# A graph attention layer on one core: the last pair of steps in pieces of 13, 9 and 4, the 99th count from the neighbour, four small gathers in the pause

## The chip, the cores and the metric

One core of a Trainium2 chip. The metric is the device time of one execution in microseconds, as the median of several runs. In the traces POOL is GpSimd, DVE is VectorE, ACT is ScalarE, PE is TensorE and SP the sync engine, which here only issues DMAs.

## What is computed

One pre-norm graph attention layer, 12,500 nodes of 128 features, 412,500 edges sorted by destination, 4 heads of 32. Cut to what matters:

```python
h = relu(layernorm(x)) @ W_node.T                       # 12500 x 4 x 32
e = edge_attr @ W_edge.T                                # 412500 x 4 x 32
att = leaky_relu(sum(concat(h[src], h[tgt], e) * a))    # 412500 x 4
m = maximum(segment_max(att, tgt), 0)
ex = exp(att - m[tgt])
denom = segment_sum(ex, tgt) + (num_edges - deg) * exp(-m)
out = x + segment_sum(ex / denom[tgt] * h[src], tgt)
```

## The kernel before

The edges are dealt to 128 partitions in order, T = 3224 each, so that a partition goes through its edges as through a sequence, one "step" per edge. A segment (all edges of one destination) is a run of steps; the running maximum and the decayed running sums are scans along the steps, and the state after a segment's last edge is the segment's result. At a partition's first and last segment the neighbours must be joined.

**Head.** For each of 98 columns of nodes (node p·98+w stands in partition p, column w) the kernel needs `cnt`, the number of edges whose destination lies below that node. ACT counts over 512 chunk ends (`count_chunks`), POOL gathers the chunk concerned (98 columns and a 99th, whose count is only needed as the upper end of the last column), DVE counts within it (`count_within`). `positions` makes from the counts the degrees, `put_i` (where a node's target term is scattered to, POOL's 98 scatters) and `get_i` (where a node's result is read). It is called for columns 0 to 90 and then for the last 7. Between them `project_copy` takes the projections of 7 columns of nodes at a time from PE's banks; SP stores these rows (`rows_scratch`), 136 numbers per node: for each head 32 values and a one, then 4 source terms. A store's buffer is one of two, so group g+2 waits for store g.

**Loop.** 13 steps are a block (KB), two blocks a pair (PB = 26), 124 pairs. For each pair POOL issues 26 indirect gathers of 128 rows into `slots`; each gather is one instruction. DVE waits for all 26 (`gather_dma`), does `logits` (source term + target term + edge term, leaky relu, running maximum M by a scan, the exponents D and D2), then for each block `sums`: multiply the gathered rows by the weights into V, and scan V with the decays A. ACT gives the weights and the decays by exponentials and copies V and M into R; SP stores R as the states of the pair (`state_scratch`). The last pair (`at_end`) goes in two pieces of 13 steps with semaphores of their own (`gather_end`), so that its first half is worked on while the second is still gathered.

**Tail.** When all states are stored, POOL gathers each partition's first state (`s_first`) and for the 98 columns the state at each node's last edge (`get_i`), 7 to a group; DVE divides, adds x, SP stores. Beside it DVE and PE join the segments that cross partitions (`tail_views`, from the last column of V and M). The queues are written out by hand per engine; every wait is on a semaphore. What POOL waits for between the last gather of the loop and the first of the tail stands in these lines:

```python
pool.wait_ge(flags_done, 1)
pool.wait_ge(zero_stored, 16)
for k in range(2):
    pool.wait_ge(store_dma[k], STORES[k])
pool.wait_ge(val_done, BLOCKS)
gather(s_first[:, :], state_d[:, :], fe_i[:, 0:1], fix_gather)
```

## Time and profile before

| | |
|---|---|
| median of 3 runs | 4960.86 us (4958.59 to 4969.13) |
| the profiled execution, its own time | 4962.95 us |
| its span in the trace | 4955.9 us |
| POOL busy | 3712.2 us, 75% |
| DVE busy | 2412.0 us, 49% |
| ACT busy | 1368.3 us, 28% |
| PE busy | 777.3 us, 16% |
| DMA | 627.97 MB, 127 GB/s in the mean |

Busy time is that of the instructions on an engine; the span runs from the first to the last instruction of the program. The 7 us between the span and the execution's own time lie before and behind it. An engine's instruction and the DMA that it issues are two things: a gather on POOL is busy while its descriptors are made, and lands later.

### The profile page before, as it was taken

What the parts mean: (1) busy time and instruction counts of PE and PEld (TensorE: products, weight loads), DVE (VectorE), ACT (ScalarE), POOL (GpSimd) and SP (SyncE); (2) the same over time, 40 slices, a digit from 0 to 9 for tenths busy, and PEclk for the clock granted to TensorE, in tenths of its full rate; (3) what the DMA queues carried; (4) which work ended last, traced back from release to release, by engine and by line L of the source; (5) the groups of instructions that cost most, each with busy time, mean ns of one, the idle gap of its engine ahead of it and who ended that gap; (6) DMA issues with size and microseconds to landing.
All of it is one profiled execution on the core that took longest, in us unless ns stands there. A gap on an engine that the chain in (4) does not pass through costs nothing.

```text
span 4955.9 us, 14358 instructions
## 1 busy us (share of the span) xinstructions
PE 777.3 (16%) x1453; PEld 390.6 (8%) x1453; DVE 2412.0 (49%) x2384; ACT 1368.3 (28%) x1021; POOL 3712.2 (75%) x3530
## 2 busy tenths in 40 slices
PE   5321111111111111111111111111111111111100
PEld 3310000000000000000000000000000000000000
DVE  7337454545445454454544545445454454544543
ACT  7013232222322222222222322223222232222320
POOL 6667777777777777777777777777777777777766
PEclk9555555555555555555555555555555555555555
DMA  7234444343443434434344343433434434343353
GB/s 250 90 132 119 140 123 128 114 137 114 126 125 114 137 114 128 123 115 137 114 127 123 114 136 114 129 121 115 137 114 128 122 115 136 114 131 120 116 170 104
DMA packets 171831, 627.97 MB, mean 127 GB/s; under 512 B 72897, under 2 KB 73666, under 8 KB 155426
## 3 DMA queue, kind: packets, MB, share of 16 engines
q0 software_dynamic: 115936, 252.37, 21.0%
q1 hardware_dynamic: 55874, 375.39, 20.1%
q14 instruction: 17, 0.14, 0.0%
q8 instruction: 4, 0.07, 0.0%
HBM read 382.66 MB, written 244.86 MB: 127 GB/s over the span
## 4 chain that ended last, share of the span: by engine, by line
POOL 70%; issue 24%; another core or an unknown queue 2%; ACT 2%; DVE 1%; PE 0%; DMA 0%; POOLq 0%; ACTq 0%; DVEq 0%; SPq 0%
POOL slots L308 69%; ACT pen L375 1%; DVE pen L482 0%; PE ae L792 0%; DVE slots L496 0%; ACT big L392 0%; ACT slots L391 0%; POOL tdst_scratch L311 0%; ACT R L421 0%; PE wexp L785 0%; DMA state_scratch<-R 0%; DVE V L636 0%; DVE slots L501 0%; DMA cols<-in_cols_dram 0%
## 5 line engine op out<-in xcount | busy, mean ns | idle before, releaser
L308 POOL DMA_INDIRECT slots<-rows_scratch,idx x3224 | 3421.5, 1061 | 1066.5 <-issue 1066.5
L803 PE MATMUL ae<-eab,w_att 128*128 128x416 f32 x992 | 650.6, 829 | 3796.2 <-DMA eab<-in_ea_dram 2539.1
L603 DVE TENSOR_TENSOR z<-slots,big 128x104 f32<-128x104 f32 (+1 forms) x125 | 43.1, 345 | 2116.3 <-DMA slots<-rows_scratch,idx 1887.3
L636 DVE TENSOR_TENSOR_SCAN V<-A,V 128x1848 f32<-128x1848 f32 x248 | 993.7, 4007 | 35.4 <-issue 4.8
L421 ACT COPY R<-V 128x1716 f32<-128x1716 f32 x248 | 777.8, 3136 | 339.1 <-DVE V L636 196.7
L417 ACT ACTIVATE A<-D 128x1848 f32<-128x1848 f32 x246 | 419.7, 1706 | 744.7 <-DVE V L636 410.3
L803 PEld LDWEIGHTS ae<-eab,w_att 128*128 128x128 f32 x992 | 296.0, 313 | 4150.4 <-issue 3384.4
L626 DVE TENSOR_TENSOR V<-slots,wexp 128x1716 f32<-128x1716 f32 x125 | 404.8, 3239 | 22.4 <-issue 21.0
L626 DVE TENSOR_TENSOR V<-slots,extra 128x1716 f32<-128x1716 f32 x123 | 398.2, 3237 | 22.0 <-issue 16.3
L438 ACT ACTIVATE wexp<-D 128x104 f32<-128x104 f32 x62 | 16.2, 261 | 1092.5 <-DVEq L621 628.8
L438 ACT ACTIVATE extra<-D 128x104 f32<-128x104 f32 x61 | 15.9, 261 | 1063.2 <-DVEq L621 631.2
L308 POOL DMA_INDIRECT V<-in_dst_dram,chunk_i x99 | 97.0, 979 | 56.6 <-issue 28.1
L311 POOL DMA_INDIRECT tdst_scratch<-tnode,put_i x98 | 95.2, 972 | 50.5 <-issue 30.0
L482 DVE TENSOR_SCALAR_CACHE_REDUCE pen<-V,cols 128x806 bf16<-128x806 int16 x99 | 100.8, 1050 | 34.7 <-DMA V<-in_dst_dram,chunk_i 24.1
L308 POOL DMA_INDIRECT slots<-state_scratch,get_i x98 | 92.8, 947 | 29.9 <-issue 29.9
L633 DVE COPY V<-V 128x132 f32<-128x132 f32 x247 | 79.4, 322 | 11.3
L646 DVE STREAM_TRANSPOSE ae_t<-ae 128x416 f32<-128x416 f32 x124 | 73.4, 592 | 0.9 <-issue 0.6
L375 ACT ACTIVATE pen<-last_b,half_n 128x512 bf16<-128x512 f32 x99 | 70.0, 713 | 9.3 <-issue 9.3
L496 DVE TENSOR_TENSOR slots<-ae,rstd 128x384 f32<-128x384 f32 x28 | 15.5, 552 | 104.3 <-remote 89.9
L612 DVE TENSOR_TENSOR_SCAN M<-pen,att 128x108 f32<-128x108 f32 (+1 forms) x123 | 47.4, 385 | 19.6 <-issue 19.1
L792 PE MATMUL ae<-w_ext,big 128*128 128x136 f32 x168 | 39.3, 416 | 86.5 <-DVE tnode L502 53.9
L608 DVE TENSOR_TENSOR z<-z,ae_t 128x104 f32<-128x104 f32 (+1 forms) x125 | 42.3, 339 | 9.3
(168 smaller groups left out, 602.3 us busy)
## 6 DMA issues: line engine op xcount, KB each, us to landing
state_scratch<-R SPq DMA_DIRECT2D x123, 1768.0 KB
eab<-in_ea_dram SPq DMA_DIRECT2D x126, 832.0 KB
slots<-rows_scratch,idx POOLq DMA_INDIRECT x3224
rows_scratch<-slots SPq DMA_DIRECT2D x14, 476.0 KB
tdst_scratch<-eab SPq DMA_DIRECT2D x4, 1612.0 KB
big<-tdst_scratch SPq DMA_DIRECT2D x8, 806.0 KB
big<-in_x_t_dram SPq DMA_DIRECT2D x14, 448.0 KB, 4.3
big<-in_x_dram SPq DMA_DIRECT2D x7, 896.0 KB
```

The lines of the kernel that those rows point to most:

```text
L308: pool.indirect_dma_start(buf, None, table, bass.IndirectOffsetOnAxis(ap=index, axis=0)).then_inc(done, 16)
L311: pool.indirect_dma_start(table, bass.IndirectOffsetOnAxis(ap=index, axis=0), buf, None).then_inc(done, 16)
L375: nc.scalar.activation(junk_a[k % 9], last_b[:, :], ACT.Sign, bias=half_n[:, k:k + 1], scale=-1.0, accum_out=sgn[:, k:k + 1])
L417: nc.scalar.activation(a_all.rearrange("p (h v t) -> p h v t", h=H, v=HB), d2.rearrange("p h (a t) -> p h a t", a=1).broadcast_to([P, H, H ...
L421: return nc.scalar.copy(R[:, k, v * KB:(v + 1) * KB, 0:VAL], vcols(v)[:, :, 1:COL].rearrange("p c t -> p t c"))
L482: nc.vector.tensor_scalar(junk_v[k % RING], ring[:, k % RING, :], cols[:, k:k + 1], None, ALU.is_lt, ALU.add, accum_out=within[:, k:k + 1] ...
L612: nc.vector.tensor_tensor_scan(M[:, u, 0:H * (n + 1)], pen_u.rearrange("p a h t -> p (a h t)"), a[:, 0:H * (n + 1)], 0.0, ALU.min, ALU.max)
L626: nc.vector.tensor_tensor(v4[:, :, :, 1:COL], slots[:, a:a + KB, 0:VAL].rearrange("p t (h v) -> p h v t", h=H), w4.rearrange("p h (a t) -> ...
L633: nc.vector.tensor_copy(vcols(v)[:, :, 0:1], vcols(1 - v)[:, :, KB:COL])
L636: nc.vector.tensor_tensor_scan(V[:, v, :], a_all, V[:, v, :], 0.0, ALU.mult, ALU.add).then_inc(scanned, 1)
L646: nc.vector.transpose(ae_t[:, :], ps_ae[k][:, 0:KB * Q]).then_inc(ae_taken, 1)
L803: last = mm(ps_ae[k][:, 0:KB * Q], w_att[:, a * P:(a + 1) * P], eab[:, k, a * KB * Q:(a + 1) * KB * Q], start=a == 0, stop=a == 3)
```

## The change

Three parts. (1) The last pair goes in three pieces, 13, 9 and 4 steps (`LAST`); `logits`, `sums`, `decay` and `copy_sums` take a piece's offset and length, the buffers for the ends get a third part, a third store is issued, and the tail reads the last piece's end. (2) The loop over counts runs over 98 columns; the 99th entry of `cnt` is copied from the first entry of the next partition by a DMA from SBUF to SBUF (for the last partition it is the constant E), and DVE waits for it in the second `positions`. (3) Behind the loop's gathers POOL issues four more gathers, of 124, 120, 112 and 64 rows, into a new tile `t_again`, and waits for them; nothing reads that tile.

```diff
+LAST = ((0, KB), (KB, 9), (KB + 9, KB - 9))
-COUNTS = (0, 2, 4, 7, 12, 20, 29, 38, 47, 56, 65, 74, 83, 92, 99)
+COUNTS = (0, 2, 4, 7, 12, 20, 29, 38, 47, 56, 65, 74, 83, 92, 98)
+PARTIAL = (124, 120, 112, 64)
...
+            sp.wait_ge(put_ready, 1)
+            sp.dma_start(cnt[0:P - 1, W:W + 1], cnt[1:P, 0:1]).then_inc(next_count, 16)
             for g in range(STEPS):
...
-                    for v in range(2):
-                        sp.wait_ge(copied, p + 1 + v)
-                        a, b = (p * 2 + v) * (KB * ROW), (p * 2 + v + 1) * (KB * ROW)
-                        sp.dma_start(state_rows[:, a:b], R[:, 1, v * KB:(v + 1) * KB, :].rearrange("p t r -> p (t r)")).then_inc(store_dma[1], 16)
+                    for e, (o, n) in enumerate(LAST):
+                        sp.wait_ge(copied, p + 1 + e)
+                        a = (p * PB + o) * ROW
+                        sp.dma_start(state_rows[:, a:a + n * ROW], R[:, 1, o:o + n, :].rearrange("p t r -> p (t r)")).then_inc(store_dma[1], 16)
...
-            for k in range(W + 1):
+            for k in range(W):
                 if k in COUNTS:
...
+            for k, n in enumerate(PARTIAL):
+                gather(t_again[0:n, k, :], tnode_d[:, :], first_i[0:n, 0:1], again_dma)
+            pool.wait_ge(again_dma, 16 * len(PARTIAL))
             pool.wait_ge(flags_done, 1)
...
             for h in range(H):
-                nc.scalar.activation(pen_end[:, :, h, 1:COL], pen_a[:, T - PB:T].rearrange("p (b t) -> p b t", t=KB), ACT.Relu)
+                for e, (o, n) in enumerate(LAST):
+                    a = T - PB + o
+                    nc.scalar.activation(pen_end[:, e, h * (n + 1) + 1:(h + 1) * (n + 1)], pen_a[:, a:a + n], ACT.Relu)
...
+                    for e, (o, n) in enumerate(LAST):
+                        act.wait_ge(d_ready, p + 1 + e)
+                        u = (p + e) % 2
+                        nc.scalar.activation(w_exp[u][:, 0:H * n], D1[:, u, 0:H * n], ACT.Exp).then_inc(w_ready, 1)
+                        decay(hk(D2_end[:, e, 0:H * (n + 1)]), n + 1)
...
+                        act.wait_ge(scanned, 2 * p + 1 + e)
+                        copy_sums(1, o, e % 2, n).then_inc(copied, 1)
...
             def positions(a, b, c):
...
+                if b == W:
+                    dve.wait_ge(next_count, 16)
                 nc.vector.tensor_tensor(deg[:, a:b], cnt[:, a + 1:b + 1], cnt[:, a:b], ALU.subtract)
```

The order of the instructions changes at three places. On SP's queue, where the head ends, before:

```order
L251 DMA idx<-in_src_dram 128x52
L255 DMA tdst_scratch<-eab 128x3224 [waits centre_done,filled]
L255 DMA tdst_scratch<-eab 128x3224 [waits centre_done] x3
L258 DMA rows_scratch<-slots 128x952 [waits rows_ready] x7
L262 DMA eab<-in_ea_dram 128x1664 [waits tdst_filled]
```

and in the changed kernel:

```order
L257 DMA idx<-in_src_dram 128x52
L261 DMA tdst_scratch<-eab 128x3224 [waits centre_done,filled]
L261 DMA tdst_scratch<-eab 128x3224 [waits centre_done] x3
L263 DMA cnt<-cnt 127x1 [waits put_ready]
L266 DMA rows_scratch<-slots 128x952 [waits rows_ready] x7
```

The copy of the counts stands ahead of all stores of the projected rows (`rows_scratch`), and waits for DVE's first `positions`.

On POOL between the loop and the tail, before (`x_first`, `rest_first` and `s_first` are one gather each, for the joins):

```order
L308 DMA slots<-rows_scratch,idx 128x136 x25
L308 DMA x_first<-in_x_dram,first_i 128x128 [waits rest_stored]
L308 DMA rest_first<-rest_scratch,first_i 128x1
L308 DMA s_first<-state_scratch,fe_i 128x136 [waits store_dma1,store_dma0,val_done,zero_stored,flags_done]
L308 DMA slots<-state_scratch,get_i 128x136 x49
```

and in the changed kernel:

```order
L316 DMA slots<-rows_scratch,idx 128x136 x25
L316 DMA x_first<-in_x_dram,first_i 128x128 [waits rest_stored]
L316 DMA rest_first<-rest_scratch,first_i 128x1
L316 DMA t_again<-tnode_scratch,first_i 124x4
L316 DMA t_again<-tnode_scratch,first_i 120x4
L316 DMA t_again<-tnode_scratch,first_i 112x4
L316 DMA t_again<-tnode_scratch,first_i 64x4
L316 DMA s_first<-state_scratch,fe_i 128x136 [waits store_dma0,store_dma1,zero_stored,val_done,flags_done,again_dma]
L316 DMA slots<-state_scratch,get_i 128x136 x49
```

The four gathers stand ahead of the waits for the stores, and the first gather of the tail waits for them too.

On DVE the end of the last pair, before (from the second piece's logits):

```order
L603 TENSOR_TENSOR z<-slots,big 128x52 [waits gather_end1]
L608 TENSOR_TENSOR z<-z,ae_t 128x52
L610 SCALAR_TENSOR_TENSOR att_end<-z 128x4x13
...
L626 TENSOR_TENSOR V<-slots,wexp 128x132x13 [waits w_ready]
L633 COPY V<-V 128x132
L636 SCALAR_TENSOR_TENSOR V<-A,V 128x1848 [waits a_ready]
L676 COPY V<-V 128x128 [waits copied]
```

and in the changed kernel, the second and the third piece:

```order
L623 TENSOR_TENSOR z<-slots,big 128x36 [waits gather_end1]
...
L647 TENSOR_TENSOR V<-slots,wexp 128x132x9 [waits w_ready]
L655 COPY V<-V 128x132
L658 SCALAR_TENSOR_TENSOR V<-A,V 128x1320 [waits a_ready]
L623 TENSOR_TENSOR z<-slots,big 128x16 [waits gather_end2]
...
L647 TENSOR_TENSOR V<-slots,extra 128x132x4 [waits copied,w_ready]
L655 COPY V<-V 128x132
L658 SCALAR_TENSOR_TENSOR V<-A,V 128x660 [waits a_ready]
L705 COPY V<-V 128x128 [waits copied]
```

What came in one piece of 13 comes in two, of 9 and 4, each with its logits, multiply and scan, and each waits for its own gathers.

## Rows read from the trace of the kernel before

**Rows 1.** The page: chain that ended last by engine, and costliest group.

```profile
POOL 70%; issue 24%; another core or an unknown queue 2%; ACT 2%; DVE 1%; PE 0%; DMA 0%; POOLq 0%; ACTq 0%; DVEq 0%; SPq 0%
...
L308 POOL DMA_INDIRECT slots<-rows_scratch,idx x3224 | 3421.5, 1061 | 1066.5 <-issue 1066.5
```

**Rows 2.** Windows: stretch, length, busy PE, PEld, DVE, ACT, POOL, PEclk, DMA share, GB/s.

```profile
3228.03:3519.23 291.20, 43.34 (x65) 19.88 (x66) 141.20 (x120) 80.62 (x48) 221.52 (x209) 0.55 0.40 123
3519.23:3810.58 291.35, 39.70 (x64) 18.37 (x64) 140.76 (x120) 80.59 (x48) 219.03 (x209) 0.56 0.40 123
3300.61:3337.71 37.10, 8.22 (x14) 3.96 (x13) 17.52 (x15) 10.07 (x6) 28.62 (x27) 0.55 0.39 121
3591.81:3628.76 36.95, 7.35 (x15) 3.46 (x13) 17.84 (x15) 10.08 (x6) 27.57 (x26) 0.61 0.40 121
305.75:4793.76 4488.01, 642.30 (x976) 291.99 (x976) 2210.17 (x1890) 1250.24 (x746) 3421.53 (x3224) 0.55 0.41 125
```

**Rows 3.** Windows: the tail's gathers on POOL, first to last.

```profile
4814.15:4937.75 123.60, 0.78 (x3) 0.47 (x3) 41.68 (x86) 3.96 (x18) 93.72 (x99) 0.50 0.49 155
```

**Rows 4.** Timeline of the last pair: start, duration, instruction, idle before and its releaser.

```profile
4781.16 1.81 POOL L308 DMA_INDIRECT slots<-rows_scratch,idx  x1 [0.30 <-issue]
...
4787.32 0.95 POOL L308 DMA_INDIRECT slots<-rows_scratch,idx  x1 [0.30 <-issue]
4787.39 3.12 ACT L421 COPY R<-V 128x1716 f32<-128x1716 f32 x1 [5.75 <-issue]
...
4792.36 1.10 POOL L308 DMA_INDIRECT slots<-rows_scratch,idx  x1 [0.30 <-issue]
...
4795.16 0.95 POOL L308 DMA_INDIRECT rest_first<-rest_scratch,first_i  x1 [0.30 <-issue]
4795.57 0.25 DVE L603 TENSOR_TENSOR z<-slots,big 128x52 f32<-128x52 f32 x1 [8.21 <-DMA slots<-rows_scratch,idx]
...
4797.61 0.22 ACT L429 ACTIVATE wexp<-D 128x52 f32<-128x52 f32 x1 [7.10 <-issue]
...
4797.86 3.24 DVE L626 TENSOR_TENSOR V<-slots,wexp 128x1716 f32<-128x1716 f32 x1 [0.31 <-ACT wexp L429]
...
4801.55 4.01 DVE L636 TENSOR_TENSOR_SCAN V<-A,V 128x1848 f32<-128x1848 f32 x1
4805.60 3.14 ACT L421 COPY R<-V 128x1716 f32<-128x1716 f32 x1 [5.93 <-DVE V L636]
...
4814.15 0.94 POOL L308 DMA_INDIRECT s_first<-state_scratch,fe_i  x1 [18.03 <-DMA state_scratch<-R]
```

**Rows 5.** Chain that ended last, its step behind the last copy.

```profile
4808.76 4.49 DMA state_scratch<-R
```

**Rows 6.** DMA issues: count, KB each, median us to landing.

```profile
state_scratch<-R SPq DMA_DIRECT2D x2, 884.0 KB
...
a_sb<-in_a_blk_dram SPq DMA_DIRECT2D x1, 6.0 KB, 2.3
```

**Rows 7.** Timeline of the head, at the end of the counting.

```profile
155.07 11.02 SPq L258 DMA_DIRECT2D rows_scratch<-slots  x2
...
157.53 0.95 POOL L308 DMA_INDIRECT V<-in_dst_dram,chunk_i  x1 [0.31 <-issue]
...
160.02 0.25 DVE L517 TENSOR_TENSOR put_i<-pick,cnt 128x91 int32<-128x91 f32 x1
...
161.06 1.00 POOL L311 DMA_INDIRECT tdst_scratch<-tnode,put_i  x1 [2.59 <-issue]
...
166.83 1.05 DVE L482 TENSOR_SCALAR_CACHE_REDUCE pen<-V,cols 128x806 bf16<-128x806 int16 x1
...
167.80 1.05 DVE L482 TENSOR_SCALAR_CACHE_REDUCE pen<-V,cols 128x806 bf16<-128x806 int16 x1
...
170.52 0.55 DVE L496 TENSOR_TENSOR slots<-ae,rstd 128x384 f32<-128x384 f32 x1
```

**Rows 8.** Waits of DVE, 150 to 300 us: total us, times, longest.

```profile
DVE slots L496 <- remote: 89.9, 7, 22.2
```

More of the change, by code:

```diff
@@ L343, in body @@
                     k = q % 2 * PB + j
-                    gather(slots[:, k, :], rows[:, :], idx[:, q // 2, k:k + 1], gather_end[j // KB] if at_end(it, q) else gather_dma[q % 2])
+                    done = gather_end[sum(j >= o for o, n in LAST) - 1] if at_end(it, q) else gather_dma[q % 2]
+                    gather(slots[:, k, :], rows[:, :], idx[:, q // 2, k:k + 1], done)
             loop(pool, body)
@@ L426, in body @@
                 if at_end(it, q):
-                    for v in range(2):
-                        act.wait_ge(d_ready, p + 1 + v)
-                        nc.scalar.activation(w_exp[1 - v][:, 0:H * KB], D1[:, 1 - v, 0:H * KB], ACT.Exp).then_inc(w_ready, 1)
-                        decay(hk(D2_end[:, v, :]))
-                        if v == 0:
+                    for e, (o, n) in enumerate(LAST):
[3 more added lines that the diff above has]
+                        decay(hk(D2_end[:, e, 0:H * (n + 1)]), n + 1)
+                        if e == 0:
                             act.wait_ge(store_dma[1], 16 * (p // 2))
-                        nc.scalar.copy(R[:, 1, v * KB:(v + 1) * KB, VAL:ROW], hk(M[:, 1 - v, 0:H * COL])[:, :, 1:COL].rearrange("p h t -> p t h"))
-                        act.wait_ge(scanned, 2 * p + 1 + v)
-                        copy_sums(1, v).then_inc(copied, 1)
+                        nc.scalar.copy(R[:, 1, o:o + n, VAL:ROW], hk(M[:, M_END[e], 0:H * (n + 1)])[:, :, 1:n + 1].rearrange("p h t -> p t h"))
+                        act.wait_ge(scanned, 2 * p + 1 + e)
+                        copy_sums(1, o, e % 2, n).then_inc(copied, 1)
                     return
@@ L478, in _ @@
             dve.sem_inc(consts, 1)
+            nc.vector.memset(cnt[:, W:W + 1], float(E))
             def count_within(k):
@@ L533, in _ @@
             dve.wait_ge(loaded_lasts, 32)
-            for k in range(W + 1):
+            for k in range(W):
                 if k % RING == 0:
@@ L630, in sums @@
                 else:
-                    if v:
+                    if o:
                         dve.drain()
-                    nc.vector.tensor_copy(vcols(v)[:, :, 0:1], vcols(1 - v)[:, :, KB:COL])
+                    nc.vector.tensor_copy(vc[:, :, 0:1], before)
                 dve.drain()
                 dve.wait_ge(a_ready, ready)
-                nc.vector.tensor_tensor_scan(V[:, v, :], a_all, V[:, v, :], 0.0, ALU.mult, ALU.add).then_inc(scanned, 1)
+                nc.vector.tensor_tensor_scan(V[:, v, 0:VAL * (n + 1)], A[:, 0:VAL * (n + 1)], V[:, v, 0:VAL * (n + 1)], 0.0, ALU.mult, ALU.add).then_inc(scanned, 1)
@@ L647, in body @@
                 if at_end(it, q):
-                    for v in range(2):
-                        dve.wait_ge(gather_end[v], 16 * KB)
-                        logits(p, k, 1 - v, v, KB, att_end, att_end, pen_end[:, v:v + 1, :, :], D2_end[:, v, :])
-                        dve.wait_ge(w_ready, p + 1 + v)
-                        if v == 0:
-                            dve.wait_ge(copied, p)
-                        sums(k, v, hk(w_exp[1 - v][:, 0:H * KB]), 2 * p + 1 + v, False)
+                    for e, (o, n) in enumerate(LAST):
+                        u = (p + e) % 2
+                        c = LAST[e + 1][1] + 1 if e + 1 < len(LAST) else COL
+                        dve.wait_ge(gather_end[e], 16 * n)
+                        logits(p, k, u, M_END[e], o, n, att_end[:, e, :], hk(att_end[:, e + 1, 0:H * c]), pen_end[:, e, 0:H * (n + 1)], D2_end[:, e, 0:H * (n + 1)])
+                        dve.wait_ge(w_ready, p + 1 + e)
+                        if e != 1:
+                            dve.wait_ge(copied, p + e // 2)
+                        m = LAST[e - 1][1] if e else KB
+                        sums(k, o, n, e % 2, hk(w_exp[u][:, 0:H * n]), 2 * p + 1 + e, vcols(1 - e % 2, m + 1)[:, :, m:m + 1])
                     return
                 dve.wait_ge(gather_dma[k], it * (16 * PB * UP // 2) + 16 * PB * (q // 2 + 1))
-                logits(p, k, k, 0, PB, att, att_end if isinstance(it, int) and it == ITERS - 1 and q == UP - 2 else att, pen[:, ds(p, 1), :, :], D2[:, k, :])
+                one_before = isinstance(it, int) and it == ITERS - 1 and q == UP - 2
+                logits(p, k, k, k, 0, PB, att, hk(att_end[:, 0, :]) if one_before else hk(att[:, :]),
+                       pen[:, ds(p, 1), :, :].rearrange("p a h t -> p (a h t)"), D2[:, k, :])
                 dve.wait_ge(w_ready, p + 1)
@@ L660, in body @@
                 for v in range(2):
-                    sums(k, v, hk(w_exp[k])[:, :, v * KB:(v + 1) * KB], it * (2 * UP) + 2 * q + 1 + v, isinstance(p, int) and p == 0 and v == 0)
+                    sums(k, v * KB, KB, v, hk(w_exp[k])[:, :, v * KB:(v + 1) * KB], it * (2 * UP) + 2 * q + 1 + v,
+                         None if isinstance(p, int) and p == 0 and v == 0 else vcols(1 - v)[:, :, KB:COL])
                 if isinstance(p, int) and p < UP:
```

96 lines of the change are left out of this document (52 added, 44 removed).

## The prediction

> **What bounds the kernel now.** I read the page first. Its chain of work that ended last is POOL for 70% and "issue" for 24%, and the costliest group by far is one line, L308: 3224 indirect gathers that POOL issues back to back, 1061 ns busy and 330 ns between two [rows 1]. The window over the main loop says the same from outside: 4488.0 us with 3224 of them, 1.392 us each, while DVE is busy for 2210 us of it and ACT for 1250 [rows 2]. POOL is also what the tail waits for: 99 gathers in 123.6 us, 1.25 us each [rows 3]. So the run is a head of 305.75 us, a loop and a tail that both go at POOL's pace, and between loop and tail a pause of 18.03 us in which POOL has nothing it may issue [rows 4]. The change can move the time only in the head, in the pause, or by making POOL's own gathers cheaper or dearer.
>
> The timeline of the last pair shows what fills the pause. POOL issues the last step's gather at 4792.36; DVE starts the second half at 4795.57, ACT gives the weights at 4797.61, DVE multiplies from 4797.86 (3.24 us) and scans from 4801.55 (4.01 us), ACT copies from 4805.60 (3.14 us) [rows 4]. Then the chain has the store: issued at 4808.76, 4.49 us [rows 5], and POOL's first gather of the tail is at 4814.15 [rows 4]. From the last gather to that one all is serial, and all but the first 5.5 us scales with the number of steps in the last piece.
>
> **Part 1: pieces of 13, 9, 4.** The first piece is as before; ACT begins to copy it at 4787.39, so DVE is free then [rows 4]. Durations go by elements. Fixed in a piece: 2.29 us from the start of the logits to the multiply, and 4801.55 − 4797.86 − 3.24 = 0.45 us between multiply and scan. I take these as unchanged for smaller pieces, though their small instructions shrink a little.
> - Piece of 9: its last step (the 22nd) is gathered at 4787.32, four gathers before the last. With the 3.21 us from issue to DVE that the last one took it starts at 4790.5. It takes 2.29 + 3.24·9/13 + 0.45 + 4.01·9/13 (1320 elements of 1848 is 10/14, 2.86) = 7.8 us, and ends at 4798.4.
> - Piece of 4: its gathers landed at 4795.57, so it waits for DVE and starts at 4798.4. DVE would be ready to multiply at 4800.7. ACT stands first in line with the copy of the piece of 9 (3.14·9/13 = 2.2 us, to 4800.6), then gives the weights; the multiply starts about 4800.85. 3.24·4/13 = 1.0, 0.45, 4.01·5/14 = 1.4: scanned at 4803.7. ACT's copy is 3.14·4/13 = 1.0: 4804.7.
> - Its store is 272 KB where 884 KB took 4.49 us [rows 5, 6]. The bounds: the gather of 128 rows of 544 bytes took 3.21 − 0.95 = 2.3 us from its end to DVE [rows 4], and 4.49. The size is nearer to the gather's 68 KB, so I take 2.8 us, by a straight line between them. The store of the piece of 9 is issued at 4800.6 and is over by 4805.1 even at 4.49. Landed: 4807.5. POOL resumed 0.9 us behind the landing before (4814.15 − 4808.76 − 4.49), so now at 4808.4.
> - The term: 4808.4 − 4814.15 = **−5.7 us**, from −4.1 (store of 4.49) to −7 (store of 2.3, and the small instructions shorter by 0.6). What follows (x loaded again, the DVE chain of the joins) hangs on the same two events and moves with them.
>
> The cost is a third set of eight small DVE instructions, a copy, a weight activation and a third store issue. All lie inside the 7.8 + 5.3 us just counted. ACT's eight more activations for the penalties (128x4 to 128x13) stand in front of the loop, where DVE's first logits wait for POOL's 26th gather; at 1.39 us each that is some 35 us of cover.
>
> **Part 2: four gathers in the pause.** POOL is free at 4795.16 + 1.25 = 4796.4. Four at 1.25 end at 4801.1 and land 2.3 later, 4803.4. The store lands at 4807.5, so 4.1 us of cover: each of the four may be 1 us dearer before POOL's wait on them is the last. Cost **0**. Nothing reads what they fetch. Their rows are not multiples of 128, which no row shows; at the price of a gather they cost 0, and at that of the dear one at 4781.16 (1.81 us and 0.3 [rows 4]) the four land at 4807.1, again 0; only beyond that do they show.
>
> **Part 3: the 99th column.** It takes away one gather of POOL in the head (157.53 was the last; POOL then waits until 161.06 for the positions anyway [rows 7], so 0), one Sign activation, and one count of DVE, which takes 0.97 us from start to next start and stands directly ahead of the positions of the last 7 columns and of the projection copies that feed POOL's scatters [rows 7]. It adds a copy of 127 elements from SBUF to SBUF on SP's queue, issued when the first positions are ready (160.3), and DVE waits for it from about 168.4 (its last count started at 167.80, now 0.97 earlier, and two small instructions follow). Before, the nearest transfers from their issue to their landing are 2.3 us (6 KB) and 4.49 (the store) [rows 5, 6]: landed by 162.6 to 164.8, hidden with 3.6 us to spare. Queued behind it on SP is the store of the first 7 columns of rows, which was issued at 155.07 [rows 7] and now goes out at about 160.8. DVE needs that buffer for the third group, at 170.52 less the 0.97 [rows 7], 169.5; 8.7 us against 4.49 for a larger store: hidden. So **−1.0 us**, between −1.4 and +6: the head has seven waits of DVE on something the trace doesn't name, 89.9 us in all [rows 8], and a reordering there can make one longer.
>
> A rule of the Trainium skill speaks against this copy ("DMA: Bandwidth & Descriptors", section on why a DMA increments its semaphore by 16): the engines used are the largest number up to 16 that divides the outer size, so 127 partitions all go on one engine. The trace has no DMA of 127 partitions. At 10.5 ns a packet, from the same page's section on bandwidth and so an estimate, 127 make 1.3 us, less than the cover, so the sum would stay.
>
> **The sum.** −5.7 − 1.0 = −6.7 us on the profiled execution's 4962.95 gives 4956.2. The median of the runs is 2.1 us lower, so 4954.2. That is 0.135%; a measurement of this kernel tells about 0.2%, 9.9 us, from no change.
>
> **What could decide instead: the loop.** The change takes one of the gathers ahead of the loop away, so each of the 3224 is one place earlier in POOL's own count. That this place matters is visible. Eight pairs (208 gathers) take 291.20 and 291.35 us in two stretches one behind the other, and within each of them one pair takes 37.10 and 36.95 [rows 2], where the other seven of 291.20 average 36.30. The pairs start at even places only (26 is even, 198 gathers stand before them); with 197 they all start at odd ones, which this trace never shows. On average over places I expect nothing, 0. One slow pair more or less in eight is 0.8 · 123/8 = 12.3 us.
>
> **The rivals.**
> - *The odd places are kinder*: no slow pair, −12.3 − 6.7, 4942. For it: the slow pair is a coincidence of one start place with the stretch where DVE begins the next pair; against it: I see only even places. From −3.2 us in the loop on (a quarter of a slow pair) the result is beyond 0.2%. Chance 0.28.
> - *They are unkinder*: one slow pair more in eight gives +12.3 − 6.7, 4966.5, no measurable change; 0.08. Three slow in eight, +24.6 − 6.7, give 4978.8, **slower**; it decides from +16.6 us in the loop, 1.1 us per eight pairs. Nothing in the rows speaks for that much. Chance 0.05.
> - *The tail pays for the four gathers*: if the odd row counts leave POOL's gathers of the tail as dear as the loop's, 1.392 instead of 1.248 [rows 2, 3], 99 of them cost +14.3, and the sum is 4968.5. Against it: the loop's surcharge goes with other engines' work there and the tail is flat now. Chance 0.04.
> - *The pause doesn't shrink*: the piece of 4 is bound by something else (the store of the piece of 9 still under way, the four gathers slow), only −1.0 remains, 4960. Chance 0.05.
> - The forecast: 0.50.
>
> **Numbers.** Range 4942 to 4966: from the kinder loop to one slow pair more; below lie perhaps 0.08, above 0.1. Faster by over 0.2%: 0.30 (the first rival, and the low end of my terms). Within: 0.64. Slower: 0.06.
>
> **What would show it.** POOL's idle before the tail's first gather, 18.0 before, is 12.3 less the four gathers' 5.0 us; DVE's scan of the last piece at 1.4 us; a store of the last 4 steps landing under 3 us; the cnt copy landed before DVE asks. The loop's window, first to last gather of 3224, tells the rest: 4488 within 3 us if I am right. Wrong would be a loop off by over 5 us, a gather in the tail above 1.3 us, or a first loop gather later than 305.

## The result and the profile after

The changed kernel is slower, by a hair: the ratio of its time to the kernel before is 1.0017, 95% interval 1.0009 to 1.0025, so 4.5 to 12.4 us; medians 4978.66 against 4967.99 us, 13 runs each. I had forecast 4954 and a range to 4966. Seven of those 24.5 us are not the change's: the forecast started from the median of 3 runs of the kernel before (4960.86), and 13 runs put it at 4967.99. The profiled execution took 4971.35 us against 4962.95, 8.4 us more; its span is 4969.5 us against 4955.9, 13.6 more. The other 5.2 us come back outside the span: the time of an execution less its span was 7.1 us before (6.6 to 7.6 in the runs of the kernel before, on the chips where it takes 4967 us or more) and is 1.8 now. No instruction is recorded there, so what shrinks is not shown, but a tail that ends 13 us later makes the kernel only some 8 us slower.

The 13.6 us between the spans split at landmarks of PoolE (POOL in the rows: GpSimd). "The loop's last gather" is the end of the last of the 3224 gathers, 4793.46 before and 4793.11 after (4791.87 + 1.24); all times with a plus below are counted from it, in every kernel.

| us | before | after |
|---|---|---|
| first loop gather | 305.75 | 304.04 |
| loop, to the end of its last gather | 4487.71 | 4489.06 |
| s_first gathered | +20.69 | +18.37 |
| TensorE's first transpose of the ends | +13.52 | +25.96 |
| last operation of the first rows' correction (x_first) starts | +49.05 | +63.75 |
| first to last of the tail's 98 gathers | 121.41 | 125.74 |
| last scatter | +152.79 | +166.14 |

The "correction" is VectorE's work on x_first, the rows of the segments that cross partitions; the "last scatter" writes these rows and is PoolE's last instruction with data. The head gave 1.7 us here, the loop took 1.35 and the end 13.35.

The windows of the changed kernel, columns as in [rows 2, 3]: the loop, and the tail's 99 gathers.

```profile
304.04:4793.41 4489.37, 637.97 (x976) 290.98 (x976) 2222.01 (x1900) 1252.78 (x751) 3418.33 (x3224) 0.55 0.41 125
4811.47:4939.97 128.50, 2.32 (x9) 1.42 (x9) 38.76 (x87) 3.87 (x18) 95.52 (x99) 0.50 0.46 143
```

The loop is the same within 1.4 us of 4488.01. The timeline of the changed kernel's third piece and pause (start, duration, instruction, idle before):

```profile
4797.75 0.17 DVE L637 COPY att_end<-M 128x4 f32<-128x4 f32 x1
4797.96 0.99 POOL L316 DMA_INDIRECT t_again<-tnode_scratch,first_i  x1 [0.30 <-issue]
...
4800.53 0.92 POOL L316 DMA_INDIRECT t_again<-tnode_scratch,first_i  x1 [0.30 <-issue]
4801.56 0.17 DVE L639 SCALAR_TENSOR_TENSOR D_end<-pen_end,dm 128x16 f32<-128x16 bf16 x1 [3.64 <-issue]
4802.94 0.19 ACT L444 ACTIVATE extra<-D 128x16 f32<-128x16 f32 x1 [3.99 <-DVEq L642]
...
4805.75 1.53 DVE L658 TENSOR_TENSOR_SCAN V<-A,V 128x660 f32<-128x660 f32 x1 [1.11 <-issue]
4807.32 1.15 ACT L435 COPY R<-V 128x528 f32<-128x528 f32 x1 [3.41 <-DVE V L658]
...
4808.54 0.17 DVE L714 MEMSET R<- 4x129 f32 x1
...
4811.47 0.95 POOL L316 DMA_INDIRECT s_first<-state_scratch,fe_i  x1 [10.02 <-DMA state_scratch<-R]
```

Three times between 4797.9 and 4805.7 VectorE stands idle at a drain for no reason that the profile names ("issue"): 3.6, 1.2 and 1.1 us. (A drain is an instruction that waits until the engine's earlier ones are through.) In the last piece of the kernel before none of them did. The pause shrinks by 2.3 us instead of 5.7. The next drain is far worse. TensorE waits for it:

```profile
4819.07 0.47 PE L840 MATMUL ae<-ident,V 128*128 128x128 f32 x1 [98.75 <-issue]
```

The memset at 4808.54 ended at 4808.71; TensorE starts 10.4 us later. Before, the same drain let TensorE begin at 4806.97, 0.1 us behind the last memset. From there VectorE stays late. Its last part, one group of seven columns, looks like this:

```profile
4856.86 0.29 DVE L768 TENSOR_TENSOR x_first<-x_first,R 128x128 f32<-128x128 f32 x1 [1.11 <-issue]
...
4871.86 0.18 DVE L776 TENSOR_TENSOR R<-R,rest 128x28 f32<-128x28 f32 x1
4874.36 0.21 DVE L778 TENSOR_TENSOR R<-R,slots 128x28 f32<-128x28 f32 x1 [2.31 <-issue]
4875.76 0.34 DVE L780 RECIPROCAL wexp<-R 128x28 f32<-128x28 f32 x1 [1.19 <-issue]
4876.47 1.09 DVE L783 TENSOR_TENSOR A<-slots,wexp 128x896 f32<-128x896 f32 x1 [0.38 <-issue]
4877.86 1.09 DVE L789 TENSOR_TENSOR big<-big,A 128x896 f32<-128x896 f32 x1 [0.30 <-issue]
4878.87 0.18 DVE L776 TENSOR_TENSOR R<-R,rest 128x28 f32<-128x28 f32 x1
```

A group takes 7.00 us, of which 2.9 are work, and 14 groups behind a correction at 4857 make 4955. PoolE's last gather is long over by then:

```profile
4954.86 1.09 DVE L789 TENSOR_TENSOR big<-big,A 128x896 f32<-128x896 f32 x1 [0.30 <-issue]
...
4959.25 1.01 POOL L319 DMA_INDIRECT out_dram<-x_first,fix_i  x1 [19.27 <-DMA out_dram<-big]
```

The kernel before has groups of 7.00 us too, but its correction was over 14 us sooner, so it caught up with the gathers: its last three groups, from 4922 on, each start within 0.1 us of the end of ACT's exponentials, and these wait for the gathers. These rows of before show its end:

```profile
4842.51 0.29 DVE L739 TENSOR_TENSOR x_first<-x_first,R 128x128 f32<-128x128 f32 x1 [1.11 <-issue]
...
4946.25 1.00 POOL L311 DMA_INDIRECT out_dram<-x_first,fix_i  x1 [8.50 <-DMA out_dram<-big]
```

So the tail has changed hands: PoolE sets its end before, VectorE after.

### The profile page after: what moved, and what is told of

Read it like the earlier page. It is cut to its first block, busy times and chain, and to the rows that moved or that the text cites. A ratio compares the mean times of both kernels' runs of the same rounds, so it can differ in the third digit from the quotient of the medians.

```text
span 4969.5 us, 14393 instructions
## 1 busy us (share of the span) xinstructions
PE 769.4 (15%) x1453; PEld 388.4 (8%) x1453; DVE 2420.8 (49%) x2394; ACT 1369.3 (28%) x1031; POOL 3714.2 (75%) x3533
## 4 chain that ended last, share of the span: by engine, by line
POOL 70%; issue 24%; ACT 2%; another core or an unknown queue 2%; DVE 1%; PE 1%; DMA 0%; POOLq 0%; DVEq 0%; ACTq 0%; SPq 0%
POOL slots L316 70%; ACT pen L387 1%; DVE pen L499 0%; PE ae L821 0%; PE wexp L814 0%; DVE slots L513 0%; PE A L804 0%; ACT big L404 0%; ACT slots L403 0%; POOL tdst_scratch L319 0%; DVE V L658 0%; DVE slots L518 0%; ACTq L388 0%; PE wexp L821 0%
## 5 line engine op out<-in xcount | busy, mean ns | idle before, releaser
L658 DVE TENSOR_TENSOR_SCAN V<-A,V 128x1848 f32<-128x1848 f32 (+1 forms) x249 | 994.1, 3992 | 36.4 <-issue 5.9
L435 ACT COPY R<-V 128x1716 f32<-128x1716 f32 (+1 forms) x249 | 778.0, 3125 | 345.7 <-issue 191.9
L647 DVE TENSOR_TENSOR V<-slots,wexp 128x1716 f32<-128x1716 f32 (+1 forms) x125 | 403.9, 3232 | 22.4 <-issue 21.4
```

The lines of the kernel that those rows point to most:

```text
L435: return nc.scalar.copy(R[:, k, o:o + n, 0:VAL], vcols(v, n + 1)[:, :, 1:n + 1].rearrange("p c t -> p t c"))
L647: nc.vector.tensor_tensor(vc.rearrange("p (h v) t -> p h v t", h=H)[:, :, :, 1:n + 1], slots[:, a:a + n, 0:VAL].rearrange("p t (h v) -> p ...
L658: nc.vector.tensor_tensor_scan(V[:, v, 0:VAL * (n + 1)], A[:, 0:VAL * (n + 1)], V[:, v, 0:VAL * (n + 1)], 0.0, ALU.mult, ALU.add).then_inc ...
```

## The experiments

Heads differ from run to run by more than the effects (the kernel before's first loop gather and that of kernels with its head lay between 299 and 324 us), so I read the distances from the loop's last gather beside each ratio. Where the change's end is unchanged (after, early_exit, after_again) they repeat to 0.15 us. Where the end is that of the kernel before they repeat less well: s_first lies between +19.43 and +20.69 in before, tail20, drains20 and head_loop, the last scatter of before, drains20 and head_loop between +152.20 and +152.79. A ratio moves less than the last scatter where VectorE ends late, for the 5 us outside the span.

**First four: which part, and per what.** two_pieces and no_partials are the changed kernel less one part (in two_pieces the tail also reads the ends from where two pieces leave them); tail20 and early20 the kernel before plus 20 tiny memsets of VectorE.

```diff
 two_pieces:  LAST = ((0, KB), (KB, KB))
 no_partials:
-            for k, n in enumerate(PARTIAL):
-                gather(t_again[0:n, k, :], tnode_d[:, :], first_i[0:n, 0:1], again_dma)
-            pool.wait_ge(again_dma, 16 * len(PARTIAL))
 tail20, on before:
             dve.drain().then_inc(end_packed, 1)
+            for k in range(20):
+                nc.vector.memset(spare[:, k:k + 1], 0.0)
 early20, on before, at the end of VectorE's body():
+                if isinstance(it, int) and it == ITERS - 1 and q == UP - 3:
+                    for m in range(20):
+                        nc.vector.memset(spare[:, m:m + 1], 0.0)
```

> The changed kernel with the last pair again in two pieces of 13 steps; the four gathers and the new source of the 99th count stay. It takes 19 instructions of VectorE's own (the third piece) out of the end. Theory A (pace): after the loop VectorE's drains end on a grid of 0.70 us and one group of nine instructions takes 7.00 us, whatever PoolE does, so VectorE gets through the code behind the loop at about one instruction in 0.70 us or a little more; the third piece costs 19 x 0.70 = 13.3 us of it. Then the correction of the first rows ends near 4843 to 4845 instead of 4857.1, PoolE's idle time before the last scatter is 8 to 10 us instead of 19.3, and the time is that of the kernel before within 4 us (ratio 0.999 to 1.001). Theory B (the four gathers held VectorE up and it never caught up): the correction still ends 10 us or more late and the ratio stays near 1.0017.

> The changed kernel without the four gathers of 124, 120, 112 and 64 rows and the wait for them. Theory A (pace of VectorE behind the loop): no instruction of VectorE goes away, so its drains in the third piece still take about 5.8 us more than they need, s_first is gathered near 4811, the last scatter starts near 4959 after 18 to 20 us of idle, and the ratio stays 1.001 to 1.0025. Theory B (the four gathers hold VectorE's drains up): the third piece runs through without those 5.8 us, s_first is gathered at 4805.5 to 4808, the last scatter starts 10 us or more earlier and the ratio is 0.998 to 1.000.

> The kernel before with 20 memsets of 128x1 on VectorE, with no drain between them, behind the drain that tells TensorE that the ends are packed. By their length they cost 20 x 0.13 = 2.6 us, of which 1.7 us lie in a wait for TensorE. Theory A (pace per instruction): the correction of the first rows ends 20 x 0.70 = 14 us later (4856 to 4858 instead of 4842.8), VectorE does not catch up with the gathers any more, and the last scatter starts 10 to 13 us later: ratio 1.002 to 1.003. Theory C (only drains are slow, whatever stands between them): correction 0 to 3 us later, same time within 2 us.

> The kernel before with the same 20 memsets of 128x1 on VectorE, at the end of the last pair but two, where VectorE waits some 10 us for the next gathers. Theory A with a store of instructions that refills while VectorE waits: nothing changes, the first slow drain stands at the same line as before (two drains behind the masks' scans) and the ratio is 0.999 to 1.001. Theory D (what matters is where a block of 128 instructions ends, so anything that shifts the code makes the end slower): the first slow drain moves 20 instructions up, into the last piece, and the time grows by 5 to 13 us, as if a third piece stood there.

| | s_first | x_first | 98 gathers | last scatter | ratio (95%) |
|---|---|---|---|---|---|
| before | +20.69 | +49.05 | 121.41 | +152.79 | |
| after | +18.37 | +63.75 | 125.74 | +166.14 | 1.0017 (1.0009 to 1.0025) |
| two_pieces | +20.62 | +49.05 | 124.04 | +155.76 | 1.0009 (1.0000 to 1.0018) |
| no_partials | +18.36 | +63.75 | 121.35 | +166.63 | 1.0018 (1.0009 to 1.0027) |
| tail20 | +19.60 | +77.05 | 124.49 | +176.08 | 1.0039 (1.0025 to 1.0052) |
| early20 | +22.00 | +60.15 | 121.24 | +162.59 | 1.0008 (0.9997 to 1.0019) |

two_pieces puts the correction back to +49.05 exactly: the third piece costs 14.7 us there. What is left of its last scatter, 3.0 us, goes with its 98 gathers, 2.6 us longer than before. no_partials changes neither s_first nor the correction. Its third piece shows the same idle time while PoolE does nothing, so the four gathers don't cause it:

```profile
4810.90 0.17 DVE L636 SCALAR_TENSOR_TENSOR D_end<-pen_end,dm 128x16 f32<-128x16 bf16 x1 [3.58 <-issue]
...
4820.79 0.95 POOL L316 DMA_INDIRECT s_first<-state_scratch,fe_i  x1 [15.56 <-issue]
...
4828.40 0.48 PE L837 MATMUL ae<-ident,V 128*128 128x128 f32 x1 [97.60 <-issue]
```

tail20 shows the thing itself. VectorE's timeline of its memsets:

```profile
4815.14 0.15 DVE L689 MEMSET spare<- 128x1 f32 x4
4815.62 0.20 DVE L689 MEMSET spare<- 128x1 f32 x6 [0.33 <-issue]
4817.84 0.06 DVE L689 MEMSET spare<- 128x1 f32 x1 [2.02 <-issue]
4819.94 0.06 DVE L689 MEMSET spare<- 128x1 f32 x1 [2.04 <-issue]
4820.64 0.06 DVE L689 MEMSET spare<- 128x1 f32 x1 [0.65 <-issue]
4822.04 0.06 DVE L689 MEMSET spare<- 128x1 f32 x1 [1.34 <-issue]
...
4829.05 0.06 DVE L689 MEMSET spare<- 128x1 f32 x1 [1.34 <-issue]
4830.45 0.06 DVE L689 MEMSET spare<- 128x1 f32 x1 [1.34 <-issue]
```

Ten come in a burst, the others at distances of 0.70, 1.40 and 2.10 us. They do nothing and cost the correction 28.0 us, 1.40 each, twice what I expected. early20 falls between my two theories: where they ran they came in a burst, and still the correction came 11.1 us later, and the first slow drains stand in the two pairs that followed. I read this as a lead that the memsets used up and that was not won back in two pairs; no row shows such a lead itself.

**Second four: fewer instructions, another exit, drains, other places.**

```diff
 wide, on after: VectorE's last part, ACT's exponentials and the stores
+WIDE = ((0, 2), (2, 2), (4, 2), (6, 1), (7, 2), (9, 2), (11, 2), (13, 1))
-            for g in range(STEPS):
+            for c, (g, m) in enumerate(WIDE):
 early_exit, on after:
-            with eng.Fori(1, ITERS - 1) as it:
+            with eng.Fori(1, ITERS - 2) as it:
 drains20, on before: dve.drain() in place of tail20's memsets
 head_loop, on before: the 20 memsets before targets(0), and in the loop after each second pair
```

> The changed kernel with VectorE's last part in 8 groups of 14 columns (two of 7, because the slots wrap at 49) instead of 14 groups of 7: the same elements, 54 instructions fewer on VectorE. In the changed kernel this part is nine instructions and 7.00 us a group, 98 us for 14 groups behind a correction that ends at 4857.1, and that makes the end (4955). Theory A (VectorE is late because each of its instructions behind the loop takes a step of 0.70 us or more): 72 instructions take 8 x 7.0 = 56 us, VectorE catches up with the gathers near 4915, and the last scatter comes 9.5 us behind the last gather as in the kernel before: 150 to 153 us after the loop's last gather instead of 166.1; ratio to the kernel before 0.998 to 1.000. Theory E (VectorE is slow by elements): groups take twice as long and nothing is gained, ratio 1.0017.

> The changed kernel with the loop left one iteration sooner: the last 8 pairs of steps stand written out instead of the last 4, nothing else differs. Theory A1 (from the exit on, instructions come at some 1.1 us each without a limit ahead, and VectorE's 134th or so is the first that is not there in time): four pairs of 36 us use 25 instructions each, that is 100 x 1.1 = 110 of 145 us, so the end starts some 35 us further ahead, the slow drains of the last piece and of the first 30 instructions behind it go, and the last scatter comes 12 us or more sooner: ratio 0.997 to 0.999. Theory A2 (VectorE works off a store of a fixed size that refills at this pace while it waits): the slow drains stand where they stood, ratio 1.001 to 1.0025.

> The kernel before with 20 drains where the 20 memsets stood (behind the drain that tells TensorE that the ends are packed). There is nothing to drain after the first, so each takes some 0.03 us by itself. Theory A (pace per instruction, whatever it does): as the memsets, the correction ends 14 to 28 us later than the 49.05 us after the loop's last gather of the kernel before, ratio 1.002 to 1.004. Theory F (memsets are a case of their own, 1.4 us each): 0 to 3 us later, ratio 1.000.

> The kernel before with 20 memsets of 128x1 on VectorE at two other places: before the first pair of steps (written out, before the loop) and after the second pair of each turn of the loop. Read is only the distance from one to the next. Theory A in its narrow form (only code written out behind the loop comes slowly): 0.01 to 0.05 us at both places. In its wide form (all code that is not in a loop comes at 0.70 us or more once the store is used up): near 0.01 in the loop, and 0.7 to 1.4 us for the last ones of the 20 before it.

| | x_first | 98 gathers | last scatter | ratio (95%) |
|---|---|---|---|---|
| wide | +63.84 | 125.65 | +155.22 | 1.0012 (1.0003 to 1.0021) |
| early_exit | +63.75 | 125.74 | +166.15 | 1.0021 (1.0012 to 1.0031) |
| drains20 | +49.05 | 121.16 | +152.20 | 1.0000 (0.9990 to 1.0009) |
| head_loop | +49.11 | 121.48 | +152.48 | one run |

With wide groups (8.4 us for twice the elements) VectorE catches up and 10.9 of the 13.4 us come back: VectorE's last part decides what the lateness costs, and that part goes by instructions more than by elements. Where the loop is left changes nothing. drains20 refutes my pace "per instruction, whatever it does", as far as the correction goes: it comes at +49.05 as before. But the drains did not pass at once. In drains20, and the last line in before:

```profile
4828.02 0.17 DVE L685 MEMSET R<- 4x129 f32 x1
4838.24 0.29 DVE L692 TENSOR_SCALAR V<-ae 128x128 f32<-128x128 f32 x1 [10.05 <-issue]
...
4864.16 0.29 DVE L741 TENSOR_TENSOR x_first<-x_first,R 128x128 f32<-128x128 f32 x1 [1.10 <-issue]
```

```profile
4808.55 0.29 DVE L690 TENSOR_SCALAR V<-ae 128x128 f32<-128x128 f32 x1 [1.66 <-PE ae L815]
```

Thirteen of the drains pass within 1.5 us, the others stand 0.70 to 2.8 us apart, and the first instruction behind them starts at +23.13 instead of +15.09. By +40 the 8 us are made up, where the 20 memsets' 28.0 us stay. So for what is lost in the end instructions with data count: a group's five at 7.00 us are 1.40 each, like the memsets; the third piece's eleven at 1.40 would be 15.4, measured 14.7. That is a count that fits, not a cause. head_loop: in the loop the 20 stand in one burst; before it the first 12 do, and the last come 0.7 us apart, half the price of those behind the loop, as here:

```profile
307.13 0.33 DVE L640 MEMSET spare<- 128x1 f32 x12
308.29 0.07 DVE L640 MEMSET spare<- 128x1 f32 x2 [0.83 <-issue]
309.73 0.06 DVE L640 MEMSET spare<- 128x1 f32 x1 [1.37 <-issue]
310.44 0.06 DVE L640 MEMSET spare<- 128x1 f32 x1 [0.65 <-issue]
```

**Third four: is it code that comes for the first time? And what do the four gathers cost?** looped writes VectorE's last part as two loops of seven turns (its waits for x stand ahead of the loops, and its products have one buffer instead of two); full4 has PARTIAL = (P, P, P, P); two kernels leave the four gathers out.

```diff
 looped, on after:
-            for g in range(STEPS):
+            for half in range(2):
+                with dve.Fori(0, 7) as g:
+                    group(half, g)
```

> The changed kernel with VectorE's last part (14 groups of 7 columns, the same instructions and sizes) written as two loops of seven turns instead of 14 times over. Theory A (code that VectorE meets for the first time comes at about 1.4 us for each instruction with data once the store is used up, code of a loop's later turns does not: in the main loop 20 memsets stood 0.01 us apart): the correction still ends 63.8 us after the loop's last gather, the first turn of each loop takes some 7 us, later ones 3.5 to 5 us, VectorE catches up with the gathers before 4900 and the last scatter comes at 151 to 155 instead of 166.1; ratio 0.999 to 1.001. Theory G (VectorE is held up by PoolE's gathers and the transfers, whatever code it runs): 7.0 us a group as before, last scatter at 166, ratio 1.0017.

> The changed kernel with four gathers of 128 rows in place of those of 124, 120, 112 and 64. In the changed kernel the 98 gathers of the end take 125.7 us, without the four gathers 121.35. Theory R (the row counts leave the rings of descriptors uneven): here 121.4, as without them. Theory O (it is the place of the 98 gathers in the row of all gathers, or their start against VectorE's, which four more of any size shift as well): 124 to 126. The time is VectorE's either way (last scatter at 166), ratio 1.0017.

> The changed kernel with the 8 wide groups on VectorE and without the four gathers: pieces of 13, 9 and 4 and the new count stay. If the last part is PoolE's again, s_first comes 18.4 us after the loop's last gather (before: 20.7), the 98 gathers take 121.4 (wide with the four gathers: 125.7), and the last scatter stands 9.4 us behind the last gather: 18.4 + 1.2 + 121.4 + 9.4 = 150.4 against 152.8 before, ratio 0.9990 to 1.0003. Had the four gathers nothing to do with the 4.3 us, it stays at 154 to 155, ratio 1.0005.

> The changed kernel with VectorE's last part as two loops and without the four gathers. As for the wide groups: 150 to 151 us from the loop's last gather to the last scatter if code of a loop comes without delay and the four gathers cost the 4.3 us, ratio 0.9990 to 1.0003; 166 if VectorE stays at 7.0 us a group.

| | x_first | 98 gathers | last scatter | ratio (95%) |
|---|---|---|---|---|
| looped | +63.75 | 141.67 | +196.82 | 1.0079 (1.0066 to 1.0092) |
| full4 | +63.75 | 126.29 | +166.15 | 1.0024 (1.0015 to 1.0034) |
| wide_no_partials | +63.75 | 121.18 | +151.91 | 0.9997 (0.9988 to 1.0006) |
| looped_no_partials | +63.75 | 141.95 | +192.16 | 1.0070 (1.0057 to 1.0083) |

looped went the wrong way by 31 us. A turn of its first loop (the first three take 7.4, 10.8 and 14.8 us) and one of its second, on VectorE:

```profile
4911.96 0.19 DVE L778 TENSOR_TENSOR R<-R,rest 128x28 f32 x1 [4.61 <-issue]
4914.66 0.21 DVE L780 TENSOR_TENSOR R<-R,slots 128x28 f32<-128x28 f32 x1 [2.51 <-issue]
4916.06 0.34 DVE L782 RECIPROCAL wexp<-R 128x28 f32<-128x28 f32 x1 [1.19 <-issue]
...
4927.26 0.19 DVE L778 TENSOR_TENSOR R<-R,rest 128x28 f32 x1 [5.15 <-issue]
...
4978.89 0.18 DVE L778 TENSOR_TENSOR R<-R,rest 128x28 f32 x1
4979.25 0.21 DVE L780 TENSOR_TENSOR R<-R,slots 128x28 f32<-128x28 f32 x1 [0.18 <-issue]
4979.53 0.34 DVE L782 RECIPROCAL wexp<-R 128x28 f32<-128x28 f32 x1
...
4982.31 0.18 DVE L778 TENSOR_TENSOR R<-R,rest 128x28 f32 x1
```

About 15.4 us (22 steps of 0.70) and 3.42 us for the same turn. The register instructions that a loop adds are recorded at mostly 0.70 us each in the slow turns and at 0.04 to 0.10 in the others, and the drains of the slow turns at 0.70, so here not only instructions with data take a step. full4 says that the four gathers' odd row counts don't matter (126.3 against 125.7), only that there are four more (121.35 without). Where VectorE isn't the bound that shows: 155.22 with them, 151.91 without. It is no surcharge on each gather. In the changed kernel the first 71 of the 98 come every 1.25 us as without the four; from there on, in each five, one comes 1.70 and the next 1.54 us behind the one before it, together 0.7 us more than two at 1.25. The dear one starts late and takes longer, as here on PoolE:

```profile
4907.77 0.95 POOL L316 DMA_INDIRECT slots<-state_scratch,get_i  x1 [0.30 <-issue]
4909.47 1.24 POOL L316 DMA_INDIRECT slots<-state_scratch,get_i  x1 [0.75 <-issue]
```

**Fourth: place of the code.** Four runs with the two loops 8, 40 and 100 instructions further on (dve.drain() in the head; the early exit). Those with 40 and 100 are one execution each.

> The kernel with VectorE's last part as two loops of seven turns, and 8 drains more in VectorE's head, where it waits anyway: its code lies 8 instructions further on, nothing else moves. Theory H (slow while PoolE gathers and 10 us after): as in the run looped, first loop 15.4 us a turn, second loop fast from about 10 us behind PoolE's last gather, last scatter at 197. Theory I (a short loop across an edge of the instruction memory is loaded anew each turn; with edges every 64 instructions, counted from the loads that the trace shows at VectorE's 736th instruction, the first loop of looped lies across one and here neither does): first turn of each loop slow, then 3.4 to 4 us a turn, last scatter at 151 to 156.

> The same with 40 drains more in VectorE's head: by theory I the first loop lies free of an edge and the second across one (at the 864th instruction), so the first loop is fast from its second turn on and the second one is slow in all its turns, 15.4 us each, after PoolE has ended too, and the last scatter comes near 60 us later than in the run with 8. Theory H: as looped.

> The kernel with the two loops, and the main loop left one iteration sooner (which by itself changed nothing), so that VectorE's two loops stand 100 instructions further on. By theory I the first is free of an edge (if edges are every 64 instructions) and the second lies across one: first fast from turn two, second 15.4 us in every turn. Theory H: as looped, first slow and second fast.

> The kernel with the two loops, 8 drains more in VectorE's head and without the four gathers. Theory I: both loops fast from their second turn on, PoolE's gathers set the end, last scatter 150 to 152 us behind the main loop's last gather (before: 152.8), ratio 0.9985 to 1.000. Theory H: as looped_no_partials, 192, ratio 1.007.

All were as looped, to 0.7 us: last scatter at +196.83, +197.52, +196.83, and +192.12 without the four gathers; ratios 1.0078 (1.0061 to 1.0094) for the first and 1.0074 (1.0060 to 1.0087) for the last. An edge in the instruction memory, as in theory I, is out. Nor is each step a transfer of instructions: the page of the changed kernel counts 17 and 4 packets of instructions in the whole run (0.14 and 0.07 MB). The first loop's end and PoolE's last gather fell together in all of them, so one run split the first loop:

```diff
+            for half, a, b in ((0, 0, 4), (0, 4, 7), (1, 0, 7)):
```

> The kernel with VectorE's last part in loops, now three: of 4, 3 and 7 turns, where it had two of 7. PoolE's last gather still waits for the seventh group. Theory H (VectorE's steps are slow while PoolE gathers, and up to some 9 us after): groups 5 to 7, in the second loop, take 15.3 us each as before, and from the second or third turn of the third loop on they take 3.4. Theory J (only the loop that comes first is slow): groups 6 and 7 take 3.4 to 9 us, and the last scatter comes some 20 us sooner than 197.

It answered another question. It ran on another chip, where **the kernel before took 4462.15 us** and this one 4460.64, one execution of each. The row of the loop's gathers on its page, which answers to [rows 1]:

```profile
L316 POOL DMA_INDIRECT slots<-rows_scratch,idx x3224 | 3054.0, 947 | 982.6 <-issue 973.8
```

And VectorE's timeline in a turn of its second loop:

```profile
4371.83 0.19 DVE L778 TENSOR_TENSOR R<-R,rest 128x28 f32 x1 [5.25 <-ACT R L478]
4372.20 0.21 DVE L780 TENSOR_TENSOR R<-R,slots 128x28 f32<-128x28 f32 x1 [0.18 <-issue]
4372.48 0.34 DVE L782 RECIPROCAL wexp<-R 128x28 f32<-128x28 f32 x1
```

No steps of 0.70 us on VectorE behind the loop: x_first at +27.28 instead of +63.75, the first group waiting for x and the others only for their gathers. And PoolE's gathers cost 1.25 us in the whole loop (32.5 us a pair from the ninth on, whatever the place) where [rows 1] have 1.39. One more run took the changed kernel itself to a further chip:

> The changed kernel, unchanged, beside the kernel before. If the kernel before takes some 4460 us here (no steps of 0.70 us): the third piece has no slow drains, s_first is gathered about 5.7 us sooner behind the loop's last gather (15 to 16 us instead of 20.7, less or more by what the pause is there), VectorE catches up with the gathers at once and the whole is 4 to 8 us faster, ratio 0.998 to 0.999. If it takes some 4970 us: the steps are there and the ratio is 1.001 to 1.0025 as before.

There the kernel before took 4990.05 and the changed one 4994.8: ratio 1.0014 (1.0005 to 1.0023), s_first +18.38, x_first +63.90, last scatter +166.29. The steps were back.

## Why the prediction was wrong

- **The step that failed** is the sentence behind the sum of part 1, "What follows (x loaded again, the DVE chain of the joins) hangs on the same two events and moves with them." It moved the other way: x_first from +49.05 to +63.75, and the end with it, +13.35 us, of which the time keeps 8.4. VectorE goes through the stretch behind the last pieces at some 1.4 us per instruction with data, which shows only from a certain instruction on; with the third piece that is a drain inside it. two_pieces shows that the third piece does it, tail20 that instructions without use do it as well. I had counted the small instructions as inside the piece's time, but what they cost stood outside it.
- **What the rows could have told.** The tail's window [rows 3] shows PoolE busy to the end and I stopped there. I did not ask how far VectorE's last part was from being the bound. It was near: 14 groups of 7.00 us from 4842.7 on end at 4940.7, and waiting for PoolE's gathers it ended at 4942.9, so 2.2 us of slack. The runs give 1.3: in the changed kernel the correction is 14.7 us later and the end 13.35, in early20 11.1 and 9.8.
- **Part 1's size**: −5.7 forecast, −2.3 measured against the one trace of before, −1.1 to −2.3 against the four with its end. The piece of 9 was sooner than forecast (scanned 4796.6, not 4798.4) and the store of the piece of 4 landed in 2.08 us, not 2.8. The three slow drains, 5.9 us, took back more.
- **Part 2, 0**: right for the pause (no_partials: s_first the same). Its rival, "the tail pays for the four gathers", was right in kind: they cost the tail's gathers 4.3 us (of its 14.3), hidden in the changed kernel behind VectorE, 3.3 us where PoolE sets the end. Its reason, the odd row counts, was wrong (full4), and so was its price for all 99.
- **Part 3, −1.0**: too small for these runs to tell: the heads scatter by 25 us. In the two traces the head has one gather of 1.25 us fewer, and from the last count's gather to the first scatter it is 4.54 us instead of 3.53 [rows 7]. The new copy was issued at 159.97, its packets of 4 bytes ran from 161.3 to 162.1, and nothing waited for it.
- **The loop, 0**: the number right, 1.4 us of 4488, the reasoning not. I took the slow pair for a matter of POOL's place in its own count. Pairs at places 1, 3, 5 and 7 modulo 8 average 36.39, 36.87, 36.08 and 36.25 us after, at 0, 2, 4 and 6 they averaged 36.32, 36.28, 36.70 and 36.30 before. The slow ones, 3 now and 4 before, are the same pairs: the fourth of each turn of the loop, which is written out for four pairs. The count moved by one and they did not, so the place is not what makes them slow. Both rivals from it, with 0.41 of the chances, rested on that reading.
- The rivals lacked the one that happened: another engine becoming the tail's bound. The chance of 0.06 for slower by over 0.2% lay almost all on the loop. By that threshold 1.0017 still counts as within, which had 0.64; but I had put it there for a gain of 6.7 us, so that is no merit of the reasoning.

What stays open: what the steps of 0.70 us are. Shown is that they don't come from the four gathers, from where the loop is left, from where the code lies (at the places tried) or from elements; that drains take them too but lose nothing in the end; that 20 memsets in the main loop come without them; and that VectorE's tail is free of them on the one chip where the whole kernel took 10% less. Whether PoolE's gathers cause them was to be settled by looped_split and was not. Against it: in the kernel before VectorE's last two groups take 3.6 and 3.2 us, nearly free of such steps, and PoolE is still gathering during the first of them. That they make the loop's gathers dear as well (1.39 is nearly 2 × 0.70) fits both chips but was not shown. Whether the change gains its few us on a chip without them was not measured.

The best version, wide_no_partials, beats the changed kernel (0.9997 against 1.0014 to 1.0017) but can't be told from the kernel before; its last scatter at +151.91 is 0.3 to 0.9 us sooner than that of the three traces with the end of before.

## What to carry to other kernels

Before shortening a wait on one engine, work out when every other engine would end if that one were free: here VectorE was 1 to 2 us from being the tail's bound, and the eleven instructions of a third piece were more than that. Splitting work into pieces multiplies small instructions, and their price is to be read from a stretch where they follow one another without cover (here 1.4 us for a memset of 128 elements behind the loop, 0.7 before it), not from their own duration of 0.06. Measure distances between landmarks of the same execution where the ends of whole runs scatter by more than the effect.

## What was not expected of the hardware

- Idle time of VectorE put down to "issue" ends on a grid of 0.70 us: distances of 0.70, 1.40 and 2.10 us between memsets that do nothing, 7.00 us for a group with 2.9 us of work, 15.3 for a turn of a small loop that also takes 3.42. It was so on all chips but one.
- The same kernel took 4967 to 4990 us on at least four chips and 4462 on another, at the same mean granted clock (0.55 to 0.57), with one gather in 1.39 us or in 1.25.
- Four more gathers ahead of 98 others made those 4.3 to 4.9 us longer, whether they had 64 to 124 rows or 128, nearly all of it behind the 66th (2.6 us in two_pieces).
- On the chips with the steps an execution of the kernel before lasted 6.6 to 7.6 us beyond its span and one of the changed kernel 1.8 to 1.9, so a difference of spans is not a difference of times.
